# Decays from GpSimd differences and ScalarE exponentials in place of VectorE scans, and split-precision input projections, in a four-batch attention and state-space kernel

## The chip, the core and the metric

The kernel runs on one core of a Trainium2 chip. The metric is the device time of one execution in microseconds (us), as the median of three runs. In the profile PE is TensorE's matmuls, PEld its weight loads, DVE is VectorE, ACT is ScalarE, POOL is GpSimd and SP is SyncE, which here only issues DMAs.

## The reference, cut to what matters

Everything is float32. The input is four batches of 128 channels by 32x32 pixels, so 1024 tokens a batch. Two blocks follow each other:

```python
# block 1: attention over the 1024 tokens of a batch
h = group_norm(x, gn_w, gn_b)                       # 8 groups
q, k, v = split(einsum('bnc,oc->bno', tokens(h), qkv_w) + qkv_b)
attn = softmax(einsum('bnc,bmc->bnm', q, k) / sqrt(128))
x = image(einsum('bnm,bmc->bnc', attn, v) @ proj_w.T + proj_b) + x

# block 2: a state-space layer with 4 heads of 32 and a state of 64
u = layernorm(tokens(x))
zxbcdt = einsum('bld,ed->ble', u, in_w)             # z 128, xBC 256, dt 4
dt = softplus(zxbcdt[..., -4:] + dt_bias)
xBC = silu(causal_conv4(xBC) + conv_b); xs, Bm, Cm = split(xBC)
A = -exp(A_log)
def step(state, inp):                               # 1024 steps
    dA = exp(dt_t * A)
    state = state * dA + (dt_t * x_t) * B_t
    y_t = einsum('bhpn,bn->bhp', state, C_t)
y = (ys + Dp * xs) * silu(z)
y = y * rsqrt(mean(y * y) + EPS) * rms_w
out = y @ out_w.T
x = x + image(out) * sigmoid(se2(relu(se1(mean_pixels(out)))))
```

## The kernel before

The four batches are called a, b, c and d. Attention of one batch and the state-space layer of the batch before it are interleaved in one instruction stream per engine. The order of all steps of all engines is one long list, `ORDER`, written out by hand; each engine walks the list and does the steps that are its own, so each engine's queue is a part of that list, in that order. A step's name is its kind, its number, its batch and, after an @, the PSUM bank that it fills: `InX1c@4` is the second half of the x projection of batch c, in bank 4.

**Attention** of a batch has 8 query tiles of 128 tokens. `S` makes the scores of a query tile against half of the keys, by three products of rounded operands: the float32 operands are split into a part rounded to fp32r and what is left (`h_hi`, `h_lo`, `q_hi`, `q_lo`), and high by high, high by low and low by high are added in PSUM. `max` (VectorE), `exp` (ScalarE), `T` (four transposes on TensorE), `pT` (ScalarE copies them out) and `PV` (TensorE, float32) follow, then `inv`, `res` and `stats` on VectorE.

**The state-space layer** works on halves of 512 tokens (n is 0 or 1) and on chunks of 128 tokens, four to a half. `u_tok` (ScalarE) normalizes, `UT` transposes, and `u` (ScalarE) copies the bank to SBUF. `InX`, `InBC` and `InZ` are one float32 product each of the weights `winC` and a half of `u`, 512 columns wide. `Dt` makes dt for four chunks by four float32 products with `u` as the weights and 128 columns of `winC` moving, of which the last four count. `dt_x` adds the bias (VectorE), `sp_exp` and the nine `sp` steps are the softplus and the log decay `la` of each token and head. `conv_x` is a convolution on VectorE, `conv_bc` one on GpSimd with terms from ScalarE.

**The decays.** Within a chunk the scan is turned into a product with a matrix L of 128 by 128 decays for each head, L[s, i] being the decay from token s to token i, and 0 where i is before s. `Cum` sums `la` up to each token on TensorE. For batches a, b and c (`by_dma(b)`): `dA` holds the decay of each token (with the first one forced to 0 by the bias `first`), and `dec` the exponential of the sums; `DAT` transposes both, `rows` copies them to SBUF, `wr` writes them to DRAM, and eight `bc` DMAs a batch read each chunk's rows back, spread over all 128 partitions, into L. There `l` turns a chunk into the matrix by one scan on VectorE (multiply by the decay, add the identity). For batch d the same matrix comes from three fp32r products into a bank (`L`: rows, minus columns, and `below`, which holds -32768 where i is before s) and an exponential on ScalarE. `to_end` takes the last column, `xend` (GpSimd) weighs the inputs, `U` and `st` make the states, `m` multiplies L by the bank of `G`, and `Y` applies it. The next batch's L is read in once `Y` of the batch before is done.

The steps that the text speaks of, as they stand in the step functions of each engine:

```python
                elif kind == "l" and by_dma(b):          # VectorE, before
                    chunk = L[:, HEADS * n:HEADS * (n + 1), :].rearrange("p a b -> p (a b)")
                    wait(dve, spread[n], b, 16)
                    V.tensor_tensor_scan(chunk, chunk, ident4[:, :, :].rearrange("p a b -> p (a b)"), 0.0, ALU.mult, ALU.add
                                         ).then_inc(l_ready.sem, 1)
```

Of the kernel before, what the change touches and what calls it, by code (L numbers as in the profile page):

```python
# [5 lines left out]
F32 = mybir.dt.float32  # L6
# [5 lines left out]
P = 128  # L12
# [21 lines left out]
FIRST_BIAS = -1000.0  # L34
# [28 lines left out]
masks0 gn_stats0 warm3 gn_mm10@4 kq_mm@0 gn_dev0 gn_mm20 gn_ve0 kq_ev warm5 gn_pow0 gn_aff0 h_hi0a h0a h1a h_lo0a  # L63
h_hi1a vp_mm@2 Q0a@4 q_hi0a vp_ev V0a@2 xob0a v0a q_lo0a V1a@1 h_lo1a S0a S1a Q1a@2 win_s win_mm@4 xob1a v1a max0a
exp0a gn_bs1 T0a@0 S2a exp1a S3a alog T1a@3 pT0a masks1 max1a PV0a pT1a PV1a exp2a T2a@0 S4a win_ev exp3a inv0a q_hi1a
res0a pT2a S5a stats0a T3a@3 q_lo1a max2a pT3a gn_bs2 PV2a PV3a gn_bs3 exp4a T4a@0 S6a exp5a S7a T5a@1 inv1a pT4a
gn_stats1 res1a pT5a max3a exp6a gn_mm11@3 exp7a PV4a PV5a S8a T6a@0 stats1a pT6a S9a T7a@2 gn_dev1 inv2a pT7a res2a
max4a PV6a PV7a exp8a stats2a inv3a xob0b exp9a T8a@2 S10a T9a@4 res3a pT8a S11a stats3a PV8a pT9a ln_ve0a gn_mm21
PV9a max5a ln_pow0a u_tok0a gn_ve1 exp10a UT0a@2 exp11a u0a S12a S13a gn_pow1 max6a T10a@3 inv4a pT10a Dt0a@1 exp12a
gn_aff1 dt_x0a exp13a T11a@4 InBC0a@0 res4a h0b sp_exp0a h1b sp0a S14a InX0a@3 S15a h_hi0b sp1a h_lo0b pT11a raw_bc0a  # L70
h_hi1b PV10a T12a@2 stats4a conv_bc0a Q0b@4 PV11a V0b@1 max7a h_lo1b inv5a exp14a q_hi0b exp15a q_lo0b sp2a sp3a
T13a@0 sp4a S0b sp5a pT12a res5a raw_x0a pT13a Q1b@4 S1b max0b q_hi1b PV12a term0a conv_x0a T14a@3 exp0b exp1b sp6a
pT14a T15a@0 PV13a q_lo1b S2b sp7a pT15a conv_x1a S3b T0b@4 inv6a stats5a sp8a T1b@0 res6a term1a max1b exp2b PV14a
PV15a exp3b inv7a pT0b stats6a Cum0a@3 S4b dec0a res7a stats7a ln_ve1a T2b@4 ln_pow1a conv_x2a S5b h0c dA0a pT1b V1b@2
conv_x3a InZ0a@0 v0b pT2b max2b u_tok1a PV0b exp4b conv_bc1a exp5b UT1a@4 S6b S7b v1b PV1b conv_bc2a u1a cd0a term2a
T3b@1 conv_bc3a DAT0a@3 Dt1a@4 max3b exp6b pT3b inv0b zv0a exp7b S8b dt_x1a T4b@2 InBC1a@4 sp_exp1a rows0a zt0a S9b
res0b PV2b max4b sp9a wr0a pT4b T5b@2 wo_s th_bc0a InX1a@3 th_x0a PV3b gate0a exp8b exp9b T6b@1 inv1b xob1b silu0a
S10b raw_bc1a sp10a pT5b stats0b sp11a res1b h1c sp12a pT6b S11b PV4b sp13a T7b@2 raw_x1a conv_bc4a pT7b sp14a T8b@1
max5b exp10b exp11b bc0a pT8b PV5b sp15a l0a T9b@3 sp16a c0a S12b conv_x4a bc1a inv2b term3a res2b S13b xob0c sp17a
# [1357 lines left out]
```

## Time and profile before

| | |
|---|---|
| median of 3 runs | 271.45 us (271.21 to 271.54) |
| the profiled execution's own time | 272.0 us |
| its span, first to last instruction | 269.8 us |
| mean granted TensorE clock | 0.993 of full speed |
| busy: PE, DVE, ACT, POOL | 254.5, 223.4, 208.1, 115.8 us |

The span is what the trace covers; 2.2 us of the execution lie outside it. Busy time is the union of an engine's instructions. Instructions of one engine overlap by some ten nanoseconds each, so the mean of one times their count is more than the busy time of an engine. Matmuls are pipelined and their ends are modelled, so how fast TensorE gets through its work is read from the chain of waits, which goes from end to end.

### The profile page before, as it was taken

The page shows a single profiled execution, that of the slowest core. Times are in us where ns is not written, and L with a number is a line of the kernel's source. Part 1 is how long each engine was busy: PE and PEld are TensorE (multiplying, and loading weights), DVE is VectorE, ACT ScalarE, POOL GpSimd, SP SyncE. Part 2 cuts the span into 40 slices and gives each one's busy share as a digit, 9 for nine tenths or more (in the row PEclk, how much of TensorE's full clock was granted, in tenths as well). Part 3 has the DMA queues.
Part 4 walks back from the last instruction along what each step waited for, and adds up shares of the span by engine and source line. Part 5 has one row for each costly group of instructions (what it writes and reads, how often), then busy time and mean ns, then how long its engine had stood idle before and what let it go on. Part 6 is the DMA issues. An engine that isn't in the chain of part 4 may idle for free. (4 is left out here: it accounts for less than half of the span.)

```text
span 269.8 us, 6198 instructions
## 1 busy us (share of the span) xinstructions
PE 254.5 (94%) x1992; PEld 224.3 (83%) x1992; DVE 223.4 (83%) x516; ACT 208.1 (77%) x414; POOL 115.8 (43%) x114
## 2 busy tenths in 40 slices
PE   2999999999999999999999999999999999989791
PEld 2989997998899889988899789888988798777680
DVE  4689746565598498999999999999989999799933
ACT  2347577989999875898887799767988889998361
POOL 8010021206402730235289742572286269758440
PEclk9999999999999999999999999999999999999997
DMA  6930000000040340000133300051005100101103
GB/s 177 395 145 4 0 0 4 2 0 0 11 149 5 108 129 2 0 2 0 38 125 112 126 2 0 6 173 64 0 2 193 45 4 2 39 0 42 39 4 117
DMA packets 10987, 15.29 MB, mean 57 GB/s; under 512 B 1515, under 2 KB 5708, under 8 KB 10956
## 3 DMA queue, kind: packets, MB, share of 16 engines
q1 hardware_dynamic: 10412, 14.69, 16.2%
q8 instruction: 17, 0.28, 0.4%
q10 hardware_dynamic: 544, 0.21, 0.3%
q14 instruction: 14, 0.11, 0.1%
HBM read 12.70 MB, written 2.20 MB: 55 GB/s over the span
## 5 line engine op out<-in xcount | busy, mean ns | idle before, releaser
L1169 PE MATMUL attn_out<-values,pT 128*128 128x129 f32 x512 | 65.6, 275 | 0.1
L1169 PEld LDWEIGHTS attn_out<-values,pT 128*128 128x128 f32 x512 | 62.6, 191 | 3.6 <-issue 1.7
L986 DVE TENSOR_REDUCE neg_max<-scores 128x1 f32<-128x1024 f32 x32 | 39.0, 1219 | 16.1 <-PE scores L1169 16.0
L655 ACT ACTIVATE probs<-scores,neg_max 128x512 f32<-128x512 f32 x64 | 42.4, 684 | 9.1 <-DVE neg_max L986 9.0
L661 ACT ACTIVATE pT<-bank 128x512 f32<-128x512 f32 x64 | 37.6, 594 | 14.0 <-PE bank L1247 13.9
L1247 PE MATMUL bank<-ident,probs 128*128 128x128 f32 x256 | 37.7, 273 | 0.0
L1247 PEld LDWEIGHTS bank<-ident,probs 128*128 128x128 f32 x256 | 30.3, 141 | 4.5 <-issue 1.4
L1169 PE MATMUL scores<-h_hi,q_hi 128*128 128x512 f32 x64 | 31.7, 496 | 0.0
L567 POOL TENSOR_TENSOR ln_rstd<-ln_var,neg_half 128x4 f32<-128x4 f32 x8 | 11.3, 1412 | 45.5 <-DVE ln_var L1008 45.5
L1079 DVE TENSOR_TENSOR_SCAN L<-L,ident 128x512 f32<-128x512 f32 x24 | 30.4, 1274 | 0.0
L581 POOL TENSOR_TENSOR pre<-pre,th 128x512 f32<-128x512 f32 x16 | 22.6, 1410 | 15.1 <-ACT pre L687 8.2
L1169 PE MATMUL scores<-h_hi,q_lo 128*128 128x512 f32 x64 | 25.2, 394 | 0.0
L1169 PE MATMUL scores<-h_lo,q_hi 128*128 128x512 f32 x64 | 25.1, 393 | 0.0
L1169 PE MATMUL bank<-u,winC 128*128 128x512 f32 x48 | 24.0, 596 | 0.0
L1093 DVE TENSOR_TENSOR L<-L,bank 128x512 f32<-128x512 f32 x32 | 20.8, 677 | 0.4 <-PE bank L1169 0.3
L1025 DVE SCALAR_TENSOR_TENSOR pre<-raw,vec,pre 128x512 f32<-128x512 f32 x21 | 18.6, 884 | 0.0
L588 POOL TENSOR_TENSOR xend<-xdt,to_end 128x512 f32<-128x512 f32 x8 | 8.9, 1108 | 20.9 <-DVE xdt L1072 12.7
L561 POOL TENSOR_TENSOR h_lo<-h,h_hi 128x512 fp32r<-128x512 f32 x6 | 8.5, 1420 | 21.7 <-ACT h_hi L638 21.7
L594 POOL TENSOR_TENSOR xs<-y,gate 128x512 f32<-128x512 f32 x7 | 9.8, 1406 | 14.2 <-DVE y L1134 14.2
L1169 PEld LDWEIGHTS scores<-h_hi,q_hi 128*128 128x128 f32 x64 | 12.2, 190 | 3.4 <-issue 1.8
L599 POOL TENSOR_TENSOR y_rstd<-ms,neg_half 128x4 f32<-128x4 f32 x8 | 10.4, 1306 | 10.1 <-DVE ms L1137 10.1
L1169 PEld LDWEIGHTS scores<-h_lo,q_hi 128*128 128x128 f32 x64 | 12.2, 190 | 2.6 <-issue 1.9
(219 smaller groups left out, 597.2 us busy)
## 6 DMA issues: line engine op xcount, KB each, us to landing
L<-decay_rows_d SPq DMA_DIRECT2D x24, 256.0 KB, 3.8
res<-in_x_tok SPq DMA_DIRECT2D x4, 512.0 KB, 7.9
out<-res SPq DMA_DIRECT2D x8, 256.0 KB, 2.0
x_all<-in_x SPq DMA_DIRECT2D x3, 512.0 KB, 8.6
decay_in<-decay_rows_d SPq DMA_DIRECT2D x24, 64.0 KB, 3.4
x_all<-in_x SPq DMA_DIRECT2D x2, 256.0 KB, 3.2
winT<-in_in_wT SPq DMA_DIRECT2D x1, 194.0 KB, 7.1
wqkv<-in_qkv_w ACTq DMA_DIRECT2D x1, 192.0 KB, 4.0
```

The source lines that it names most:

```text
L567: pool.tensor_tensor(ln_rstd[:, four], ln_var[:, four], neg_half[:, four], ALU.pow).then_inc(ln_rstd_ready.sem, 1)
L581: pool.tensor_tensor(pre[:, 1, half_of(n)], pre[:, 1, half_of(n)], term(b, n, j), ALU.add).then_inc(tap["bc"].sem, 1)
L594: pool.tensor_tensor(y2[:, half], y[:, half], gate[:, half], ALU.mult).then_inc(y2_ready.sem, 1)
L599: pool.tensor_tensor(y_rstd[:, four], ms[:, four], neg_half[:, four], ALU.pow).then_inc(y_rstd_ready.sem, 1)
L655: act.activation(probs[:, i % 2, half_of(h)], scores[:, half_of(h)], ACT.Exp, bias=neg_max[:, i:i + 1]).then_inc(exp_done.sem, 1)
L661: act.activation(pT[:, i % 2, QUAD * h:QUAD * (h + 1), :], bank[:, :].rearrange("p (a b) -> p a b", a=QUAD), ACT.Copy).then_inc(pT_ready.s ...
L986: V.tensor_reduce(neg_max[:, n:n + 1], scores[:, :], AX.X, ALU.max, negate=True).then_inc(max_ready.sem, 1)
L1025: V.scalar_tensor_tensor(pre[:, 0, half_of(n)], raw[:, 0, n * HALF + j:(n + 1) * HALF + j], vec[:, CONV_X + j:CONV_X + j + 1], pre[:, 0, h ...
L1079: V.tensor_tensor_scan(chunk, chunk, ident4[:, :, :].rearrange("p a b -> p (a b)"), 0.0, ALU.mult, ALU.add).then_inc(l_ready.sem, 1)
L1093: V.tensor_tensor(M[:, HEADS * n:HEADS * (n + 1), :], L[:, HEADS * n:HEADS * (n + 1), :], bank[:, tile(c)].unsqueeze(1).broadcast_to([P, H ...
L1169: return T.matmul(o, w, v, start=start, stop=stop)
L1247: last = T.transpose(bank[:, tile(c)], probs[:, i % 2, tile(QUAD * h + c)], ident[:, :])
```

## The change

For batches a, b and c the VectorE scan `l` is replaced. The rows spread into L are now the running sums and not the decays: `dA` copies them out of the `Cum` bank, as it did for batch d. A new step `ld` on GpSimd does two passes over a chunk: it subtracts the sum at s and adds `below`. `l` is then an exponential on ScalarE. The projections use rounded parts: `u_hi` (the old `u`, written as fp32r), `u_lo` (a new VectorE step, the bank minus `u_hi`, held for one half only), `win_hi` and `win_lo`. Each of `InX`, `InBC`, `InZ` is three fp32r products of 512 columns instead of one float32 product. `Dt` is eight fp32r products with the tokens as weights and 8 or 4 columns moving instead of four float32 products of 128 columns, and `dt_x` has a second addition. The transposed bank is now released by `u_lo`. `wqkv` shares SBUF with `zv`. `ORDER` is new as a whole (left out here; it has the same steps and the 32 new ones); no DMA is added or removed.

```diff
@@ VectorE @@
-                    for h in range(HEADS):
-                        V.tensor_copy(ident4[:, h, :], ident[:, :])
...
-                    V.tensor_scalar(first[:, :], ident[:, 0:1], FIRST_BIAS, None, ALU.mult)
...
-                    V.tensor_copy(winC[:, :], bank[:, 0:INPROJ])
+                    step_done(V.tensor_copy(win_hi[:, :], bank[:, 0:INPROJ]))
+                    step_done(V.tensor_tensor(win_lo[:, :], bank[:, 0:INPROJ], win_hi[:, :].bitcast(F32), ALU.subtract))
+                    V.tensor_copy(win_dt[:, 0:HEADS], win_hi[:, 3 * P:INPROJ].bitcast(F32))
+                    V.tensor_copy(win_dt[:, HEADS:2 * HEADS], win_lo[:, 3 * P:INPROJ].bitcast(F32))
...
+                elif kind == "u_lo":
+                    wait(dve, u_hi_ready, b, n + 1)
+                    for use in ("InX", "InBC", "InZ", "Dt"):
+                        wait(dve, filled[use], b - 1, n + 2)
+                    bank = take(dve, b, "UT", n)
+                    V.tensor_tensor(u_lo[:, :], bank[:, :], u_hi[:, half].bitcast(F32), ALU.subtract).then_inc(u_lo_ready.sem, 1)
                 elif kind == "dt_x":
...
+                    V.tensor_tensor(by_head, parts[:, :, HEADS:2 * HEADS], by_head, ALU.add).then_inc(dtx_ready.sem, 1)
...
-                elif kind == "l" and by_dma(b):
-
-                    chunk = L[:, HEADS * n:HEADS * (n + 1), :].rearrange("p a b -> p (a b)")
-                    wait(dve, spread[n], b, 16)
-                    V.tensor_tensor_scan(chunk, chunk, ident4[:, :, :].rearrange("p a b -> p (a b)"), 0.0, ALU.mult, ALU.add
-                                         ).then_inc(l_ready.sem, 1)
@@ GpSimd @@
+                elif kind == "ld":
+                    wait(pool, spread[n], b, 16)
+                    wait(pool, dA_ready, b, n // QUAD + 1)
+                    pool.wait_ge(below_ready.sem, 1)
+                    chunk = L[:, HEADS * n:HEADS * (n + 1), :]
+                    c = n % QUAD
+                    pool.tensor_tensor(chunk, chunk, dA[:, n // QUAD, HEADS * c:HEADS * (c + 1)].unsqueeze(2)
+                                       .broadcast_to([P, HEADS, P]), ALU.subtract).then_inc(ld_step.sem, 1)
+                    wait(pool, ld_step, b, n + 1)
+                    pool.tensor_tensor(chunk, chunk, below[:, :].bitcast(F32).unsqueeze(1).broadcast_to([P, HEADS, P]), ALU.add
+                                       ).then_inc(ld_ready.sem, 1)
@@ ScalarE @@
-                    act.activation(u[:, half], bank[:, :], ACT.Copy).then_inc(u_ready.sem, 1)
+                    act.activation(u_hi[:, half], bank[:, :], ACT.Copy).then_inc(u_hi_ready.sem, 1)
...
-                    if by_dma(b):
-                        act.activation(dA[:, n, 0:R], la[:, n, :], ACT.Exp, bias=first[:, :], scale=1.0 / A_SCALE
-                                       ).then_inc(dA_ready.sem, 1)
-                    else:
-
-                        bank = take(act, b, "Cum", n)
-                        act.activation(dA[:, n, 0:R], bank[:, 0:R], ACT.Copy, scale=1.0 / A_SCALE).then_inc(dA_ready.sem, 1)
+                    wait(act, ld_ready, b - 1, QUAD * (n + 1))
+                    bank = take(act, b, "Cum", n)
+                    act.activation(dA[:, n, 0:R], bank[:, 0:R], ACT.Copy, scale=1.0 / A_SCALE).then_inc(dA_ready.sem, 1)
...
-                elif kind == "l" and not by_dma(b):
+                elif kind == "l" and by_dma(b):
+                    wait(act, ld_ready, b, n + 1)
+                    chunk = L[:, HEADS * n:HEADS * (n + 1), :]
+                    act.activation(chunk, chunk, ACT.Exp).then_inc(l_ready.sem, 1)
+                elif kind == "l":
@@ TensorE @@
-                    mm(bank[:, :], winC[:, tile(k)], u[:, half]).then_inc(done, 1)
+                    mm(bank[:, :], win_hi[:, tile(k)], u_hi[:, half], True, False)
+                    mm(bank[:, :], win_lo[:, tile(k)], u_hi[:, half], False, False)
+                    wait(pe, u_lo_ready, b, n + 1)
+                    mm(bank[:, :], win_hi[:, tile(k)], u_lo[:, :], False, True).then_inc(done, 1)
...
                     for c in range(QUAD):
-                        last = mm(bank[:, tile(c)], u[:, tile(QUAD * n + c)], winC[:, INPROJ - P:INPROJ])
+                        at = c * P
+                        mm(bank[:, at:at + 2 * HEADS], u_hi[:, tile(QUAD * n + c)], win_dt[:, :], True, False)
+                        last = mm(bank[:, at:at + HEADS], u_lo[:, tile(c)], win_dt[:, 0:HEADS], False, True)
```

## Rows read from the trace of the kernel before

**Rows 1.** The page's first part: busy us, share of the span, instructions.
```profile
PE 254.5 (94%) x1992; PEld 224.3 (83%) x1992; DVE 223.4 (83%) x516; ACT 208.1 (77%) x414; POOL 115.8 (43%) x114
```

**Rows 2.** Busy time by stretch: us, PE, PEld, DVE, ACT, POOL, clock, DMA share, GB/s.
```profile
76.00:214.00 138.00, 137.56 (x1103) 121.40 (x1102) 129.40 (x274) 115.78 (x234) 63.14 (x47) 1.00 0.19 60
...
255.00:270.00 15.00, 7.66 (x87) 6.89 (x86) 6.49 (x14) 5.42 (x14) 4.54 (x4) 0.87 0.14 54
```

**Rows 3.** The chain of waits from 154 to 206 us: start, us, what.
```profile
156.33 0.68 PE scores L1169 x3
157.01 0.86 PE bank L1169 x2
...
160.53 0.89 PE bank L1169 x8
...
183.47 1.01 PE bank L1169 x32
...
205.26 0.39 PE bank L1169 x4
```

**Rows 4.** TensorE in order of time at the same places.
```profile
156.85 1.02 PE L1169 MATMUL bank<-u,winC 128*128 128x512 f32 x2
...
205.10 0.55 PE L1169 MATMUL bank<-ones,o_sum 128*128 128x1 f32 x4
```

**Rows 5.** VectorE's groups from 76 to 214 us: busy us, mean ns, idle before.
```profile
L1079 DVE TENSOR_TENSOR_SCAN L<-L,ident 128x512 f32<-128x512 f32 x24 | 30.4, 1274 | 0.0
...
L1025 DVE SCALAR_TENSOR_TENSOR pre<-raw,vec,pre 128x512 f32<-128x512 f32 x15 | 14.1, 938 | 0.0
...
L847 DVE TENSOR_TENSOR sp_s<-sp_s,dte 128x16 f32<-128x16 f32 x4 | 0.7, 165 | 0.0
```

**Rows 6.** VectorE in order of time, 145 to 149 us.
```profile
145.32 2.22 DVE L1079 TENSOR_TENSOR_SCAN L<-L,ident 128x512 f32<-128x512 f32 x1
147.46 1.70 DVE L1025 SCALAR_TENSOR_TENSOR pre<-raw,vec,pre 128x512 f32<-128x512 f32 x1
```

**Rows 7.** GpSimd in order of time, 127 to 150 us, idle and its releaser in brackets.
```profile
133.55 1.28 POOL L594 TENSOR_TENSOR xs<-y,gate 128x512 f32<-128x512 f32 x1 [5.17 <-DVE y L1134]
...
138.60 1.92 POOL L567 TENSOR_TENSOR ln_rstd<-ln_var,neg_half 128x4 f32<-128x4 f32 x1 [1.12 <-DVE ln_var L1008]
140.50 2.05 POOL L581 TENSOR_TENSOR pre<-pre,th 128x512 f32<-128x512 f32 x1
142.52 1.27 POOL L555 TENSOR_TENSOR res<-res,ob_row 128x512 f32<-128x512 f32 x1
...
145.19 1.26 POOL L561 TENSOR_TENSOR h_lo<-h,h_hi 128x512 fp32r<-128x512 f32 x1
146.41 2.19 POOL L594 TENSOR_TENSOR xs<-y,gate 128x512 f32<-128x512 f32 x1
```

**Rows 8.** Groups of the whole span that the new instructions are costed by.
```profile
L709 ACT ACTIVATE th<-pre 128x512 f32<-128x512 f32 x8 | 5.0, 629 | 0.6 <-DVE pre L1025 0.6
...
L982 DVE SCALAR_TENSOR_TENSOR q_lo<-bank,col,q_hi 128x512 fp32r<-128x512 f32 x8 | 5.9, 742 | 2.3 <-ACT q_hi L644 2.3
...
L1012 DVE TENSOR_TENSOR dtx<-bank,dtb 128x16 f32<-128x16 f32 x8 | 1.3, 166 | 2.0 <-PE bank L1169 2.0
...
L588 POOL TENSOR_TENSOR xend<-xdt,to_end 128x512 f32<-128x512 f32 x8 | 8.9, 1108 | 20.9 <-DVE xdt L1072 12.7 <-DVE to_end L1088 7.0 <-issue 1.0
```

**Rows 9.** Who waited for whom, whole span: us in total, times, longest.
```profile
ACT pT L661 <- PE bank L1247: 13.9, 19, 2.6
...
ACT probs L655 <- DVE neg_max L986: 9.0, 13, 2.0
```

**Rows 10.** The chain of waits from 228 to 246 us.
```profile
232.43 0.19 DVE dtx L1012
...
239.13 0.18 ACT dA L747
...
240.32 3.65 PE bank L1169 x26
```

More of the change, by code:

```diff
@@ L62 @@
 ORDER = """
[L63 to L67, printed above, removed]
@@ L128 @@
[L128 to L132 removed]
+masks0 warm3 gn_stats0 gn_mm10@0 kq_mm@1 gn_dev0 gn_mm20 gn_ve0 kq_ev gn_pow0 warm5 gn_aff0 vp_mm@0 h0a h_hi0a win_s
@@ new lines @@
+h_lo0a h_hi1a alog Q0a@1 q_hi0a h1a vp_ev h_lo1a q_lo0a V0a@4 S0a S1a win_mm@0 v0a masks1 max0a gn_bs1 V1a@3 exp0a
+xob0a exp1a v1a xob0b S2a S3a T0a@3 T1a@4 pT0a max1a exp2a Q1a@2 PV0a pT1a win_ev S4a PV1a inv0a res0a T2a@4 exp3a S5a
+T3a@3 pT2a q_hi1a max2a PV2a xob1b pT3a exp4a gn_bs2 PV3a inv1a T4a@4 gn_bs3 res1a S6a exp5a S7a gn_stats1 max3a pT4a
+T5a@0 PV4a pT5a exp6a q_lo1a gn_mm11@3 PV5a T6a@0 exp7a pT6a stats0a S8a S9a gn_dev1 inv2a T7a@4 res2a max4a pT7a
+stats1a exp8a PV6a PV7a exp9a stats2a T8a@2 pT8a S10a T9a@0 inv3a pT9a S11a xob0c res3a gn_mm21 stats3a PV8a ln_ve0a
@@ new lines @@
+yo_dx1c zt0d c0d Y1c@4 conv_x3d UT1d@2 bt0d dA_rows0d DAT0d@1 Out0c@3 u1d y1c th_x0d dA_T0d L0d@4 Dec0d@1 u_lo1d
+Dt1d@0 o0c decay0d InX1d@3 xs0d g1c fin0b sq1c dt_x1d l0d sp_exp1d L1d@0 os0c Ss1c@1 raw_x1d sp9d InBC1d@4 sp10d l1d
+sp11d XsT0d@0 conv_x4d L2d@3 gate0d sp12d ms1c raw_bc1d term3d conv_bc4d sp13d conv_x5d sp14d L3d@1 l2d sp15d G0d@4
+sp16d conv_x6d l3d y_pow1c sp17d Cum1d@2 dec1d InZ1d@3 xdt0d dA1d to_end0d dA_rows1d conv_bc5d term4d cd1d zt1d m0d
+xend0d DAT1d@0 store0b dA_T1d m1d zv1d Out1c@2 term5d U0d@1 conv_x7d st0d o1c conv_bc6d L4d@3 L5d@0 L6d@2 conv_bc7d
@@ L210, in build @@
         winTg = sb("winTg", [P, INPROJ])
-        winC = sb("winC", [P, INPROJ])
+        win_hi, win_lo = sb("win_hi", [P, INPROJ], F32R), sb("win_lo", [P, INPROJ], F32R)
+        win_dt = sb("win_dt", [P, 2 * HEADS], F32R)
         dtb = sb("dtb", [P, HEADS])
@@ L241, in build @@
         u_tok = sb("u_tok", [P, TILES, P])
-        u = sb("u", [P, TOKENS])
+        u_hi, u_lo = sb("u_hi", [P, TOKENS], F32R), sb("u_lo", [P, HALF], F32R)
         raw = sb("raw", [P, 2, PAD + TOKENS])
@@ L267, in build @@
         dA = sb("dA", [P, 2, P])
-        first = sb("first", [P, 1])
         decay_rows = sb("decay_rows", [2 * R, 2, P])
@@ L372, in released @@
         def released(kind, n, b):
-            one = {"V": v_ready, "T": pT_ready, "UT": u_ready, "InX": raw_ready["x"], "InBC": raw_ready["bc"], "Dt": dtx_step,
+            one = {"V": v_ready, "T": pT_ready, "UT": u_lo_ready, "InX": raw_ready["x"], "InBC": raw_ready["bc"], "Dt": dtx_ready,
                    "XsT": xdt_ready, "BT": BT_ready, "U": st_ready, "Yo": yo_ready, "Y": y_ready, "Ss": ms_ready,
```

151 lines of the change are left out of this document (74 added, 77 removed).

## The prediction

> **What bounds the kernel now.** I read the page's first part, then busy time by stretch, then the chain of waits, then the groups. TensorE is busy 254.5 of 269.8 us [rows 1]. From 76 to 214 us, the stretch that holds all 24 scans of `l`, it is busy 137.6 of 138, VectorE 129.4, ScalarE 115.8 and GpSimd 63.1 [rows 2]. Matmuls overlap, so a busy TensorE could still be waiting; the chain of waits decides. From 154 to 206 us it is nearly all TensorE, at the same pace for the same work each time [rows 3]: the kernel's middle is bound by TensorE's work. At about 136 to 149 us it is not: GpSimd works there instruction behind instruction, and the gated product `xs<-y,gate` that `Ss` needs comes last in its queue [rows 7]. From 232 to 240 us one half of batch d is a dependent chain, from `dt_x` through the softplus to `dA` [rows 10], and after 255 us TensorE is busy only half of the time [rows 2].
>
> **In projections.** One float32 product of 512 columns is two instructions and 0.86 us on the chain; the three fp32r products of a score tile are 0.68 [rows 3, 4]. The new projection is three such products. I take 0.70, as a score tile that follows a float32 group may cost: 24 x (0.86 - 0.70) = **-3.8 us**. Bounds: -4.3 at 0.68, and -2.9 (0.74) if now and then the third product waits for `u_lo`.
>
> **Dt.** Eight instructions of 128 columns take 0.89 us now [rows 3]. Eight with 8 or 4 columns are new, each with 128 columns of weights to load. The nearest row is the four of one column, `o_sum`: 0.39 [rows 3, 4], so 0.78 for eight: 8 x (0.78 - 0.89) = **-0.9 us**. Bounds: 0 (the weight load sets the pace whatever moves) and -5.1 (the pace of 32 products with 32 columns of weights, 1.01 us [rows 3], 0.25 for eight). I take the row with full weights.
>
> The Trainium skill, "TensorE: Matmul & The Clock Gate", section LDWEIGHTS, gives a load P/1.2 ns, 107 ns for 128 columns, whatever the type; by it eight take 0.86 us, the term is -0.2 instead of -0.9, and the sum below would be 0.7 us higher. Rows show 98 ns for one-column instructions.
>
> **VectorE.** It loses 24 scans, 30.4 us [rows 5], and four copies of `ident4` in the first microseconds, before its data have landed (0). It gains eight `u_lo`, a subtraction from a bank like `q_lo`, at 742 ns: 5.9 us, and eight additions like `dtx` at 166 ns: 1.3 us [rows 8]. In the stretch 129.4 becomes some 103. It was not what TensorE waited for on the chain, so I take 0 for the relief as such.
>
> **ScalarE.** 24 exponentials from SBUF to SBUF, at 629 ns like the tanh (5.0 us busy for 8, so 0.62 each [rows 8]): 15.0 us, less 0.7 for six `dA`, which become copies. In the stretch 115.8 + 14.3 = 130.1 of some 134 us. Hidden behind TensorE: **0**, but the cover is 4 us thin (rival A). Bounds 0 and the whole 14.3.
>
> **GpSimd.** 24 x 2 passes. The second is like a full addition, 1.27 us; the first has a broadcast operand like `xend`, 1.11 [rows 7, 8]: 24 x 2.38 = 57 us. The stretch goes from 63 to 120 of 134. Behind each `ld` in the same queue stand `conv_bc`, `ln_pow`, `g` (which `Ss` and `Out` need), `xend` and `y_pow`. Each chunk of L also comes later: 2.4 + 0.6 us instead of 1.27, and a half of four chunks takes GpSimd 9.5 us. A batch has some 55 us of TensorE time, mostly attention of the next batch, that covers this. **0**, bounds -3 and +9 (rivals C and B).
>
> **The two engines' common path.** At 145.32 a scan takes 2.22 us, not 1.2: GpSimd's `h_lo` began at 145.19 and ends at 146.45. GpSimd's `xs` then starts at 146.41 and takes 2.19 instead of 1.28, to just after the scan's end, and the next convolution tap on VectorE takes 1.70 [rows 6, 7]. Instructions of both engines with two operands in SBUF go in turns, and with some 0.15 us of overlap at each handover. The scan was one of these; both passes of `ld` are too, and `u_lo` is not (one operand is a bank). In the stretch 15 VectorE groups of this kind, the first with 30.4 us, the last with 0.7 [rows 5], sum to 70 us, and GpSimd has 63: 133 of 138. The change takes 30 away and adds 57.
>
> The Trainium skill, "SBUF — State Buffer", section Who interferes with whom, has this as a rule: a VectorE instruction with two SBUF inputs and a GpSimd one that reads SBUF exclude each other, and the second "fully blocks" until the first ends. The trace agrees (2.22 instead of 1.2 us), except for the 0.15 us at a handover. By the rule without that overlap the stretch needs 160 us of a path that offers 134; rival B is what it would do.
>
> **The end.** Batch d keeps its decays. But `u_lo1d` comes between `u_hi` and `Dt1d`, and the second addition before the softplus, on the chain of [rows 10]: 0.74 + 0.17 = **+0.9 us**. Bounds 0 (if the new order starts it earlier) and +1.5 with waits.
>
> **Start.** `win_lo` and `win_dt` are four small VectorE instructions beside the first scores: 0. `win_s` now stands before `h_lo0a`, and could hold it for its DMA: 0 to +0.8; I take 0, since two V products no longer come before the first scores.
>
> **Sum.** 269.8 - 3.8 - 0.9 + 0.9 = 266.0 us of span. 2.2 us lie outside it: 268.2. The profiled execution is at 272.0, 0.55 above the median, so I forecast 267.6 for the median; a measurement tells 0.2%, 0.5 us, from no change.
>
> **Rivals.**
> A. *ScalarE becomes the bound.* It makes exponentials and copies that TensorE waits for next, and it waits itself: 13.9 us for transposes and 9.0 for maxima over the span [rows 9]. In the stretch it was idle 22.2 us. If more than 4 us of that stays, ScalarE decides. If half stays (11.1), the stretch is 130.1 + 11.1 = 141.2, 3.2 longer than before. Outside of it 1.5 of the projections' gain and +0.9 remain: 271.45 + 3.2 - 1.5 + 0.9 = **274.0**. For it: 97% load. Against: VectorE carried 94% here without stalling TensorE.
> B. *GpSimd's queue and the common path.* Without waits counted twice (24 scans at 1.2, 15 taps at 0.74 and GpSimd's at 1.27 take some 16 us off the 133), the path needs 117 - 29 + 57 = 145 us where 138 were. +7, and outside -0.6: **278**. Decisive once GpSimd's queue in the stretch passes 134. Against: the power steps are long but read four elements, and handovers overlap; `ld` can also spread beyond the stretch.
> C. *More gain.* On the chain at 138 to 148.6 us GpSimd's own waits for VectorE are 0.9 (`ln_pow`), 0.8, 0.9 and, for a power step between, 0.4 over what such instructions take alone [rows 7]. Without scans 3 us of this go, and a lighter VectorE delivers `y` and `ln_var` sooner: **264.6**, down to 262.
> D. *Nothing is seen.* The order changes, stalls of 4 us come with the thin ScalarE cover and use up the projections' gain: **271.4**.
>
> **How the numbers follow.** Forecast 0.45 (its own range 265.5 to 269.5), C 0.20, D 0.08, A 0.16, B 0.11. Faster by over 0.2% are the forecast, C and a little of D and A: 0.68; within 0.2%: 0.08; slower 0.24. The range holds 8 in 10 if it runs from 262.5 to 274.5: C almost whole, A whole, and B left out.
>
> **What would show it.** Three fp32r products with `u_hi` and `u_lo`, 0.70 us a group on the chain; `Dt` 0.78 for eight; 24 exponentials at 0.6 us; 48 passes at 1.1 and 1.3 us or, where turns are taken, up to 2.2; convolution taps on VectorE above 0.94; TensorE's busy time in 76 to 214 still near 100%. Wrong if ScalarE's busy time is above 96% over a long stretch while TensorE idles (A), if GpSimd's is (B), or if TensorE's chain in the middle is the same length although each projection is shorter (D).

## The result, and the profile after

The kernel after takes **274.12 us** (median of 4 runs, 273.77 to 274.48); the kernel before, on the same chip, 271.5. The ratio is 1.0082, 95% interval 1.0046 to 1.0119: slower by 2.6 us where 3.9 us faster was forecast. Ratios here are over undisturbed runs only, so they can differ a little from a ratio of the medians. The spans of the profiled executions are 272.0 and 269.8 us; 1.8 and 2.2 us of the executions lie outside them.

The page's first part of the kernel after, beside [rows 1]:

```profile
PE 253.1 (93%) x2016; PEld 228.3 (84%) x2016; DVE 226.0 (83%) x506; ACT 218.6 (80%) x438; POOL 167.9 (62%) x162
```

30.4 us of scans are gone from VectorE and 7 us of `u_lo` and additions have come; of the 223.4 us before, 200 should be left. It is busy 226.0, more than before. That is the first thing to explain. Busy time by stretch, beside [rows 2] (us, PE, PEld, DVE, ACT, POOL, clock, DMA share, GB/s):

```profile
76.00:214.00 138.00, 134.62 (x1111) 123.02 (x1109) 123.24 (x260) 124.79 (x254) 112.29 (x91) 1.00 0.20 62
```

VectorE 123.2 instead of the 103 of the forecast; TensorE no longer 100% (134.6 of 138). VectorE's groups over the whole span (busy us, mean ns of one, idle before):

```profile
L862 DVE TENSOR_TENSOR sp_s<-sp_s 128x112 f32<-128x112 f32 x8 | 6.1, 757 | 0.1
L864 DVE TENSOR_TENSOR_SCAN sp_sum<-sp_s,sp_coef 128x128 f32<-128x128 f32 x8 | 6.0, 748 | 0.1
L1027 DVE TENSOR_TENSOR u_lo<-bank,u_hi 128x512 fp32r<-128x512 f32 x8 | 5.5, 690 | 2.5 <-ACT u_hi L687 2.4
...
L859 DVE TENSOR_TENSOR sp_s<-sp_s,dte 128x16 f32<-128x16 f32 x8 | 4.8, 594 | 0.2
L855 DVE TENSOR_SCALAR sp_den<-dte 128x16 f32<-128x16 f32 x8 | 4.0, 497 | 1.6 <-ACT dte L744 1.6
L875 DVE TENSOR_SCALAR la<-la_raw 128x16 f32<-128x16 f32 x8 | 3.7, 463 | 0.1
...
L1035 DVE TENSOR_TENSOR dtx<-bank,dtx 128x16 f32<-128x16 f32 x8 | 1.4, 175 | 0.3
L1032 DVE TENSOR_TENSOR dtx<-bank,dtb 128x16 f32<-128x16 f32 x8 | 1.3, 167 | 0.8 <-PE bank L1183 0.7
```

`sp_s<-sp_s,dte` has 16 columns and took 165 ns [rows 5]; it now takes 594. Nine of the ten groups of the softplus, which touch SBUF alone, take 1.3 to 3.6 times what they took; the tenth, the reciprocal, takes the same (242 and 246 ns). Together they are busy 39 us where they were busy 20. `dtx`, of the same size but with a bank as an operand, is where it was (166 and 167 ns; its new second addition takes 175), and `u_lo`, also from a bank, takes 690, less than the 742 that it was costed at. VectorE and then GpSimd in order of time show what holds the small ones up:

```profile
152.04 0.24 DVE L857 RECIPROCAL sp_s<-sp_den 128x16 f32<-128x16 f32 x1
152.31 1.30 DVE L859 TENSOR_TENSOR sp_s<-sp_s,dte 128x16 f32<-128x16 f32 x1
153.65 1.07 DVE L862 TENSOR_TENSOR sp_s<-sp_s 128x112 f32<-128x112 f32 x1
154.64 1.21 DVE L998 TENSOR_REDUCE neg_max<-scores 128x1 f32<-128x1024 f32 x1
```

```profile
150.82 1.40 POOL L591 TENSOR_TENSOR L<-L,dA 128x512 f32<-128x512 f32 x1
152.30 1.27 POOL L594 TENSOR_TENSOR L<-L,below 128x512 f32<-128x512 f32 x1
153.53 1.05 POOL L601 TENSOR_TENSOR xend<-xdt,to_end 128x512 f32<-128x512 f32 x1
```

The product of 16 columns starts at 152.31, the mask's pass at 152.30: it ends at 153.61, just behind the pass (153.57), after 1.30 us instead of 0.17. The next small one, at 153.65, does the same with `xend`. Behind them waits the maximum of a score tile, which the exponentials, the transposes and TensorE wait for in turn. I add up, for all of VectorE's instructions that read and write SBUF alone, with one input or with two, the time beyond the shortest fifth of their form: 12.2 us before, **32.4 us** after. This sum is called VectorE's waits from here on; how the forms are grouped moves it by about 1 us, alike in all versions. Nearly all of the rise is in the softplus.

TensorE's own work went as forecast for the projections, though not for `Dt`. In order of time:

```profile
140.75 0.63 PE L1261 MATMUL bank<-ident,probs 128*128 128x128 f32 x4
141.13 0.48 PE L1183 MATMUL bank<-u_hi,win_hi 128*128 128x512 f32 x1
141.45 0.40 PE L1183 MATMUL bank<-u_hi,win_lo 128*128 128x512 f32 x1
141.68 0.40 PE L1183 MATMUL bank<-u_lo,win_hi 128*128 128x512 f32 x1
...
145.33 0.25 PE L1183 MATMUL bank<-win_dt,u_hi 128*128 128x8 f32 x1
...
146.12 0.25 PE L1183 MATMUL bank<-win_dt,u_lo 128*128 128x4 f32 x1
```

A projection runs from the end of the transposes (141.38) to 142.08, 0.70 us. The eight small products of `Dt` start 0.79/7 = 0.113 us apart, so eight take 0.90. Taking TensorE's work as the sum of the usual distances between the ends of its products, it went from 237.1 to 233.5 us (-3.6), and what its ends lag behind that went from 22 to 28. Both figures rest on modelled ends and on how the products are grouped, so they are good to 1 or 2 us. By the rows above and [rows 3], the projections alone save 24 x (0.86 - 0.70) = 3.8 us. So the saving came, and more stalls than it. GpSimd's and ScalarE's new groups:

```profile
L594 POOL TENSOR_TENSOR L<-L,below 128x512 f32<-128x512 f32 x24 | 33.6, 1401 | 1.9
L591 POOL TENSOR_TENSOR L<-L,dA 128x512 f32<-128x512 f32 x24 | 26.6, 1109 | 10.3 <-DMA L<-decay_rows_d 10.3
```

```profile
L768 ACT ACTIVATE L<-L 128x512 f32<-128x512 f32 x24 | 15.1, 638 | 0.3 <-POOL L L594 0.3
```

### The profile page after: what moved, and what is told of

Read it like the earlier page. It is cut to its first block and busy times, and to the rows that moved or that the text cites. A ratio compares the mean times of both kernels' runs of the same rounds, so it can differ in the third digit from the quotient of the medians.

```text
span 272.0 us, 6372 instructions
## 1 busy us (share of the span) xinstructions
PE 253.1 (93%) x2016; PEld 228.3 (84%) x2016; DVE 226.0 (83%) x506; ACT 218.6 (80%) x438; POOL 167.9 (62%) x162
## 5 line engine op out<-in xcount | busy, mean ns | idle before, releaser
L594 POOL TENSOR_TENSOR L<-L,below 128x512 f32<-128x512 f32 x24 | 33.6, 1401 | 1.9
L591 POOL TENSOR_TENSOR L<-L,dA 128x512 f32<-128x512 f32 x24 | 26.6, 1109 | 10.3 <-DMA L<-decay_rows_d 10.3
L569 POOL TENSOR_TENSOR ln_rstd<-ln_var,neg_half 128x4 f32<-128x4 f32 x8 | 9.4, 1178 | 35.2 <-DVE ln_var L1020 35.2
L1183 PE MATMUL scores<-h_hi,q_hi 128*128 128x512 f32 x64 | 28.5, 445 | 0.2 <-ACT probs L668 0.2
L583 POOL TENSOR_TENSOR pre<-pre,th 128x512 f32<-128x512 f32 x16 | 21.2, 1325 | 8.2 <-ACT pre L700 4.6
L1183 PE MATMUL scores<-h_hi,q_lo 128*128 128x512 f32 x64 | 25.4, 397 | 0.1
L1183 PE MATMUL scores<-h_lo,q_hi 128*128 128x512 f32 x64 | 25.2, 393 | 0.0
L1045 DVE SCALAR_TENSOR_TENSOR pre<-raw,vec,pre 128x512 f32<-128x512 f32 x21 | 17.7, 843 | 0.1
L601 POOL TENSOR_TENSOR xend<-xdt,to_end 128x512 f32<-128x512 f32 x8 | 10.2, 1274 | 10.3 <-DVE to_end L1102 3.9
L768 ACT ACTIVATE L<-L 128x512 f32<-128x512 f32 x24 | 15.1, 638 | 0.3 <-POOL L L594 0.3
L1183 PEld LDWEIGHTS scores<-h_hi,q_lo 128*128 128x128 f32 x64 | 12.0, 188 | 3.2 <-DVE q_lo L994 0.5
L700 ACT ACTIVATE pre<-raw,vec 128x512 f32<-128x512 f32 x16 | 13.2, 825 | 0.0
```

The lines of the kernel that those rows point to most:

```text
L583: pool.tensor_tensor(pre[:, 1, half_of(n)], pre[:, 1, half_of(n)], term(b, n, j), ALU.add).then_inc(tap["bc"].sem, 1)
L591: pool.tensor_tensor(chunk, chunk, dA[:, n // QUAD, HEADS * c:HEADS * (c + 1)].unsqueeze(2) .broadcast_to([P, HEADS, P]), ALU.subtract).th ...
L594: pool.tensor_tensor(chunk, chunk, below[:, :].bitcast(F32).unsqueeze(1).broadcast_to([P, HEADS, P]), ALU.add).then_inc(ld_ready.sem, 1)
L700: act.activation(pre[:, k, half], raw[:, k, half], ACT.Identity, scale=vec[:, at:at + 1], bias=vec[:, at + TAPS:at + TAPS + 1]).then_inc(t ...
L768: act.activation(chunk, chunk, ACT.Exp).then_inc(l_ready.sem, 1)
L1045: V.scalar_tensor_tensor(pre[:, 0, half_of(n)], raw[:, 0, n * HALF + j:(n + 1) * HALF + j], vec[:, CONV_X + j:CONV_X + j + 1], pre[:, 0, h ...
```

## Experiments on GpSimd's passes

The diffs from here on are shortened: semaphores and declarations are left out.

**Passes that read nothing.** In the kernel after both passes of `ld` become five memory sets of nearly the same total length (2.30 us a chunk instead of 2.51), so the decays are left out:

```diff
-pool.tensor_tensor(chunk, chunk, dA..., ALU.subtract)
-pool.tensor_tensor(chunk, chunk, below..., ALU.add)
+for k in range(4):
+    pool.memset(chunk, 0.0)              # each waits for the one before
+pool.memset(chunk[:, 0, :], 0.0)
```

> The changed kernel with the two GpSimd passes of each ld replaced by five memsets of the same chunk, which take about the same GpSimd time (2.2 to 2.4 us a chunk) and read no SBUF; L then holds zeros, so the decays are left out. Path theory: VectorE no longer waits for them; its small softplus instructions fall back to their lengths alone, its busy time from 226 to 205-210 us, and the time to 268 to 271. ScalarE theory and order theory: VectorE's waits were hidden, 273.5 to 274.5 as it is. GpSimd's queue as the bound: also unchanged, as its load is.

268.28 us (268.24 to 268.76), ratio 0.9868 (0.9834 to 0.9902). GpSimd is busy 163.1 us, 4.8 less than in the kernel after; VectorE's waits fall from 32.4 to 17.3 us. The page's first part, then VectorE's group of the example above:

```profile
PE 250.7 (94%) x2016; PEld 227.9 (85%) x2016; DVE 212.3 (80%) x506; ACT 217.9 (82%) x438; POOL 163.1 (61%) x234
```

```profile
L857 DVE TENSOR_TENSOR sp_s<-sp_s,dte 128x16 f32<-128x16 f32 x8 | 1.4, 172 | 0.2
```

The same order, the same ScalarE and TensorE work, nearly the same queue, and 5.8 us less. Some 0.5 us of it may be the shorter queue: that is my estimate, from the version with four subtractions below, where 33 us more of GpSimd's passes go with 3.2 us. The rest is the price of the reads. What is left is 3.2 us faster than before, near the forecast (267.6): the kernel after loses its gain, and more, to GpSimd's reads.

The memory sets are not free for VectorE either. In order of time, VectorE and then GpSimd:

```profile
157.76 0.16 DVE L871 TENSOR_TENSOR la_raw<-dt,a_neg 128x16 f32<-128x16 f32 x1
157.96 0.36 DVE L873 TENSOR_SCALAR la<-la_raw 128x16 f32<-128x16 f32 x1
```

```profile
157.18 1.11 POOL L591 MEMSET L<- 128x512 f32 x2
```

A product with two inputs runs beside the memory set at its own length. The one-input instruction behind it, 0.17 us when alone, ends at 158.32, just behind the memory set (158.29). `sp_den` does the same in this run (354 ns), `la` and the copy `to_end` in the run with memory sets in the old order (501 and 431 ns). So VectorE's two-input instructions wait for GpSimd's reads, and its one-input `TENSOR_SCALAR` and `COPY` also for its writes; the reciprocal waits for neither (at most 0.25 us in the kernel after, with up to 1.3 us of an addition left). By kind, VectorE's waits for one-input instructions are some 5 us with either form of `ld`; the fall is in the others.

**The same in the kernel before.** There, 24 further GpSimd passes, one behind each decay step of the first three batches, once as sums of two views of the identity, once as three memory sets of together 1.36 us; nobody reads the result. Scans, projections and the rest stay (the set-up weights share space with `gate` to make room).

```diff
+elif kind == "gx":
+    pool.tensor_tensor(idle[:, :, :], view, view, ALU.add)     # view: ident, broadcast to 512 columns
```
```diff
+elif kind == "gx":
+    for width in (2, HEADS, HEADS):
+        pool.memset(idle[:, 0:width, :], 0.0)
```

> The kernel before with 24 more GpSimd passes of 512 columns (the sum of two views of the identity, written to a place that nobody reads), one behind each decay step of the first three batches, and the set-up weights in shared space. It is the price of GpSimd's work in the old order, with VectorE's scans kept. Waits over SBUF as the cause: VectorE's waits rise by 24 x 0.4 to 0.8 = 10 to 19 us less what GpSimd waits instead, and the time by 2 to 6, to 273.5 to 277.5. If GpSimd's passes are free as long as the queue has room (43% busy): 271.5 to 272.

> The same as the run before with each added pass as three memory sets of together 1.3 us: the same time on GpSimd's queue at the same places, nothing read from SBUF. If the cost is the waits over SBUF, 271.3 to 272.3; if it is GpSimd's queue that makes its later work late, the same as the run before.

Reads: 287.24 us (ratio 1.0565, 1.0538 to 1.0592). Memory sets: 277.95 (1.0238, 1.0222 to 1.0255). First the page's line of the reads, then that of the memory sets:

```profile
PE 259.9 (91%) x1992; PEld 227.1 (80%) x1992; DVE 237.3 (83%) x516; ACT 208.9 (73%) x414; POOL 143.7 (50%) x138
```

```profile
PE 256.7 (93%) x1992; PEld 225.8 (82%) x1992; DVE 224.5 (81%) x516; ACT 208.5 (75%) x414; POOL 143.6 (52%) x186
```

GpSimd is busy 143.6 to 143.7 us in both; the reads alone cost 9.3 us, and VectorE's waits are 25.4 against 14.9. Both expectations were too low, and the second shows what I had not expected: 6.4 to 6.6 us for 33 us of work in a queue that is 43% busy before [rows 1]. Work in the queue has a price even where nothing is read. Part of it is that what stands behind it comes later, as this row of the waits with memory sets shows, which the kernel before does not have:

```profile
PE bank L1200 <- POOL h_lo L586: 2.2, 1, 2.2
```

How much of it is that, and how much the one-input instructions that wait for the memory sets, was not taken apart.

**One input instead of two.** The mask is put on with an affine select, the result is the same:

```diff
-pool.tensor_tensor(chunk, chunk, below..., ALU.add)
+pool.affine_select(out=chunk, in_=chunk, compare_op=ALU.is_ge, fill=-BELOW, base=0,
+                   pattern=[[0, HEADS], [1, P]], channel_multiplier=-1)
```

> The kernel after with GpSimd's second pass (the addition of the mask, two inputs) written as an affine select, one input, that puts the same -32768 in the same places: the result is the same. In the set-up such a select took 0.29 to 0.38 us for 128 columns, so 0.9 to 1.4 us for 512, about as long as the pass it replaces. That VectorE's waits come from GpSimd passes with two inputs from SBUF: VectorE's waits fall from 32 us by a third to a half and a third to a half of the 5.8 us come back, 271 to 272.5. If any read of SBUF by GpSimd holds VectorE up: no change, 274, less only by what the select is shorter.

271.51 us median (269.39 to 274.25 over 11 runs), ratio 0.9978 (0.9952 to 1.0005): about 1% or 2.8 us faster than the kernel after, and not to be told from the kernel before. GpSimd's two groups:

```profile
L591 POOL TENSOR_TENSOR L<-L,dA 128x512 f32<-128x512 f32 x24 | 26.6, 1109 | 9.2 <-DMA L<-decay_rows_d 9.2
...
L594 POOL TENSOR_SCALAR_AFFINE_SELECT L<-L 128x512 f32<-128x512 f32 x24 | 17.9, 744 | 3.6
```

The select takes 744 ns where the addition took 1401, which I had not foreseen (0.9 to 1.4), and VectorE's waits are 24.7 (the profile is of the longest of the 11 runs, 274.25 us). Both the length and the inputs changed, so the times do not say whether one input holds VectorE up less than two. The trace does, VectorE and then GpSimd:

```profile
161.07 0.40 DVE L871 SCALAR_TENSOR_TENSOR dt<-dtx,sp_log 128x16 f32<-128x16 f32 x1
```

```profile
160.81 0.63 POOL L594 TENSOR_SCALAR_AFFINE_SELECT L<-L 128x512 f32<-128x512 f32 x1
```

`dt` takes 0.15 to 0.18 us alone and here ends at 161.47, just behind the select (161.44). In this run and the next, six two-input instructions of VectorE start well inside a select, and all six end 23 to 27 ns behind it. So the select holds VectorE up as an addition does; what helps is that it is half as long. The next version has the subtraction as four instructions of one input and a number per partition:

```diff
+for h in range(HEADS):
+    pool.tensor_scalar(chunk[:, h, :], chunk[:, h, :], dA[:, n // QUAD, at:at + 1], None, ALU.subtract)
```

> As the one before, and the first pass as well: four GpSimd subtractions of one number per partition from 128 columns in place of one subtraction with two inputs of 512 columns, same result. Passes with two inputs as the cause: near the run with memory sets, 268.5 to 270.5, if the four take about as long as the one (1.11 us). If they are much longer (over 1.6 us), GpSimd's queue becomes late and it gives part back, 270 to 274. Any read as the cause: 274 or more.

274.73 us, ratio 1.0139 (1.0095 to 1.0183). The row:

```profile
L593 POOL TENSOR_SCALAR L<-L,dA 128x128 f32<-128x128 f32 x96 | 61.7, 660 | 8.1 <-DMA L<-decay_rows_d 8.1
```

Four take 2.6 us instead of 1.1. VectorE's waits are 21.6 although the passes are on for 33 us longer than in the version with the select alone. In the trace, two-input instructions of VectorE that start inside such a subtraction, with 0.35 to 0.56 us of it left, take 0.16 to 0.29 us: it holds them up a little or not at all. But GpSimd is busy 186 us, and the longer queue costs more than that gives.

**The select first**, so that `dA` is needed only by the second pass:

> The kernel after with the select as GpSimd's first pass, on the landed rows, and the subtraction of the row decays as its second: the same result and the same work as the select version (269.4 to 272.2), but one fewer wait ahead of the first pass. If that wait matters: 269 to 270; if not, as the select version, 270 to 271.5.

271.77 us, ratio 1.0029 (0.9992 to 1.0066): no better than the select behind the subtraction. Waiting for `dA` ahead of the first pass costs nothing that can be measured.

**One pass, and the column's decay as the bias of the exponential** (the mask is still put on by GpSimd):

```diff
-pool.tensor_tensor(chunk, chunk, dA..., ALU.subtract)
+for h in range(HEADS):
+    act.activation(chunk[:, h, :], chunk[:, h, :], ACT.Exp, bias=dA[:, n // QUAD, at:at + 1], scale=-1.0)
```

> The kernel after with one GpSimd pass over each chunk of decays instead of two: the decay of the row is stored negated, GpSimd only puts the mask on, and the exponential takes the column's decay as its bias, four exponentials of 128 columns instead of one of 512. GpSimd has 24 x 1.1 = 27 us less, all of it reading SBUF; ScalarE has 24 x (4 x 0.28 - 0.63) = about 12 us more. That GpSimd's passes over SBUF make VectorE wait: about half of the 5.8 us that all passes cost comes back, so 269 to 271.5. ScalarE as a bound would take it back: 275 to 280.

280.71 us, ratio 1.0317 (1.0252 to 1.0382): where 269 to 271.5 was expected if the reads alone decide, and 275 to 280 if ScalarE does. VectorE's waits fall to 25.2 us, but the exponentials are twice what they were:

```profile
L767 ACT ACTIVATE L<-L,dA 128x128 f32<-128x128 f32 x96 | 30.7, 409 | 0.1
```

ScalarE is busy 232.4 instead of 218.6. Its spare time is as thin as rival A said: 14 us more of it, with 27 us of GpSimd's passes gone, make the kernel 6.6 us slower than the kernel after.

**Less of ScalarE.** Was it the bound already in the kernel after? Exponentials of 4 of the 512 columns:

```diff
-act.activation(chunk, chunk, ACT.Exp)
+act.activation(chunk[:, :, P - 1:P], chunk[:, :, P - 1:P], ACT.Exp)
```

> The changed kernel with the 24 exponentials over L taken of 4 columns of 512 (the last of each head), the rest of L left as logarithms, so the decays are wrong there. ScalarE loses some 10 us of its 218.6. ScalarE theory (rival A): 270 to 271.5. Path theory: ScalarE was covered, 273 to 274.3.

276.18 us median (273.53 to 278.29), ratio 1.0121 (1.0066 to 1.0176); ScalarE is busy 209.7 (in the profiled run, the longest, 278.29 us). 9 us less of it bring no gain. The run with memory sets says the same from the other side: ScalarE is busy 129.2 of 138 us there in the stretch, and TensorE 137.7.

## Experiments on the projections and on VectorE's length

**Parts in the old order.** The kernel before with the new projections, `Dt` included, `u_lo` at its full size, a step of its own behind `u`; scans and order stay.

```diff
-mm(bank[:, :], winC[:, tile(k)], u[:, half])
+mm(bank[:, :], win_hi[:, tile(k)], u_hi[:, half], True, False)
+mm(bank[:, :], win_lo[:, tile(k)], u_hi[:, half], False, False)
+mm(bank[:, :], win_hi[:, tile(k)], u_lo[:, half], False, True)
```

> The kernel before, in its old order and with its VectorE scans, and only the projections by rounded parts (u_lo inserted behind u, held for both halves, weights of the set-up sharing space). TensorE does 3.6 us less work, VectorE gets 5.5 us of u_lo. If the loss of the whole change is the decays' doing (path theory: GpSimd's passes over L make VectorE's instructions with two SBUF operands wait), this gains: 268.5, between 267 and 270. If u_lo and the second addition at the end and the waits for u_lo eat what the products save, it is 271 to 273.

277.31 us, ratio 1.0218 (1.0172 to 1.0264), where 267 to 270 was expected: with TensorE's work down as in the kernel after, 5.7 us slower than before. The waits have a row for it, of TensorE for `u_lo` (us, times, longest):

```profile
PE bank L1204 <- DVE u_lo L1042: 3.3, 3, 1.3
```

Two more versions take `u_lo` apart: 16 of its 512 columns, and no `u_lo` at all (the third product reads `u_hi`, so the low part of `u` is left out; no wait, no step).

```diff
-V.tensor_tensor(u_lo[:, half], bank[:, :], u_hi..., ALU.subtract)
+V.tensor_tensor(u_lo[:, n * HALF:n * HALF + R], bank[:, 0:R], u_hi..., ALU.subtract)
```
```diff
-wait(pe, u_lo_ready, b, n + 1)
-mm(bank[:, :], win_hi[:, tile(k)], u_lo[:, half], False, True)
+mm(bank[:, :], win_hi[:, tile(k)], u_hi[:, half], False, True)
```

> The kernel before with the projections by parts in its own order, as in the first experiment, but the subtraction that forms u_lo runs over 16 of 512 columns (the other columns of u_lo are zeros written in the set-up, so the low part of u is left out of most of the product). TensorE does the same work; VectorE has 8 x (0.69 - 0.1) = 4.7 us less. That VectorE bounds beside TensorE: the 4.7 us come back nearly whole, 277.3 - 4 to 277.3 - 6, so 271 to 273; if TensorE's 3.6 us then count as well, down to 268. The rival, that the projections' third product waiting for one more step costs the time whatever its length: 276 to 277.5.

> The kernel before with the projections by parts, but no u_lo at all: the third product reads u_hi again (so the low part of u is left out of the result), TensorE does the same work as with parts, and nobody waits for u_lo or holds the bank for it. If the forecast's term of -3.8 us is on the path: 268 to 269 (3.6 less than before, about 0.5 of the second addition back). If TensorE's saving is not on the path: 271 to 272.

273.95 us (1.0087, 1.0048 to 1.0126) and 273.25 us (1.0045, 1.0018 to 1.0073). `u_lo`'s length costs some 3.4 of the 5.7 us. But even with no `u_lo`, TensorE's saving does not arrive: its work is 4.1 us less than before (233.0), its lag 27.3 instead of 22. Neither expectation held.

**No `u_lo` in the kernel after**, the same edit:

> The same on the kernel after: no u_lo, the third product reads u_hi. It prices u_lo in the new order: VectorE has 5.5 us less. VectorE with its waits as a bound there: 268.5 to 271.5. Nothing on the path: 273.5 to 274.5.

273.18 us (1.0103, 1.0046 to 1.0159): 0.9 us below the kernel after by the medians, not below it by the ratios. In the new order no price of `u_lo` can be told from the noise.

**Scans back.** The kernel after, its order and its projections, with the scans of before:

> The changed kernel in its new order, with the VectorE scans and the exponential of dA back and no ld; the projections stay by parts. GpSimd's busy time falls from 168 to some 105 us, ScalarE's by 15, VectorE's waits from 32 to some 12 us, but the scans add 29. Path theory: VectorE's sum is the same either way (226 + 29 - 20 = 235 busy), so 271 to 275 in an order not made for scans. Order theory (the new order itself is what loses): 274 or more. If neither, as in the old order with parts: 268 to 270.

284.04 us, ratio 1.0438 (1.0396 to 1.0481). That is 9.9 us slower than the kernel after. The new order was laid out for a light VectorE; with the scans back ScalarE waits for maxima 21.8 us (9.0 before [rows 9]):

```profile
ACT probs L659 <- DVE neg_max L993: 21.8, 21, 3.0
```

**Less of VectorE in the kernel before.** Scans over 256 of their 512 columns, and over 16:

```diff
-V.tensor_tensor_scan(chunk, chunk, ident4..., 0.0, ALU.mult, ALU.add)
+V.tensor_tensor_scan(chunk[:, 0:256], chunk[:, 0:256], ident4[:, 0:2, :]..., 0.0, ALU.mult, ALU.add)
```

> The kernel before with the 24 decay scans over 256 of their 512 columns (half of the decays are left as the exponentials of the first column alone), so VectorE has 24 x 0.55 to 0.6 = 13 to 14 us less and nothing else changes. My forecast took VectorE's relief as 0: then 270.5 to 271.5. If VectorE was a bound beside TensorE in the kernel before, a third to two thirds of it comes back: 262 to 267.

> The kernel before with the 24 decay scans over 16 of their 512 columns (so the decays are left out nearly whole): VectorE has 24 x 1.1 = 26 us less and nothing else changes. If VectorE's length is off the path, as the half scans say (-0.4 for 11 us less): 270 to 271.5. If the second half of it counts: 266 to 269.

271.09 us (0.9964, 0.9932 to 0.9996) and 271.16 us (0.9991, 0.9970 to 1.0012). In the second VectorE is busy 21.6 us less:

```profile
PE 254.2 (94%) x1992; PEld 224.7 (83%) x1992; DVE 201.8 (75%) x516; ACT 208.1 (77%) x414; POOL 107.6 (40%) x114
```

and nothing comes of it; VectorE only waits longer for scores (24.0 us by the waits, 16.0 before). The half scans gave 0.4%, at the edge of their interval. By itself VectorE's length was hardly on the path. **Both savings at once:**

> The same with the projections by parts without u_lo (TensorE 3.6 us less; the low part of u left out as well). TensorE and VectorE pacing each other by turns: the two together give what neither gives alone, 265 to 268. A third thing that sets the pace: no less than the better of the two alone, 270 to 273.

269.66 us, ratio 0.9931 (0.9915 to 0.9948), between what I expected of TensorE and VectorE pacing each other (265 to 268) and of a third thing (270 to 273). The parts without `u_lo` are worth +0.45% with the full scans and -0.6% with the short ones: 1.6 of TensorE's 4 us arrive once VectorE is light, none of them while it is not. Through which wait is not shown: ScalarE waits 9.3 us for maxima in both versions.

**Float32 projections in the kernel after**, and in the version with the select:

```diff
-mm(bank[:, :], win_hi[:, tile(k)], u_hi[:, half], True, False)      # and the two behind it
+mm(bank[:, :], winC[:, tile(k)], u[:, half])
```

> The kernel after with the float32 projections of before in place of the parts: no u_lo and no second addition, so VectorE has about 7 us less and TensorE 3.6 us more; decays by GpSimd and ScalarE and the order stay. VectorE with its waits as the bound: faster than after, 268 to 272. TensorE as the bound: 277 to 278.

> The kernel after with the select and the float32 projections of before: VectorE has 7 us less than in the select version, TensorE 3.6 us more. VectorE as the main bound of what is left: 268 to 270. Projections neutral, as they were without the select (275.2 against 274.1): 270.5 to 272.5.

275.18 us (1.0127, 1.0056 to 1.0198) and 274.34 us (1.0105, 1.0072 to 1.0138). With both passes as they are, the parts are worth 0.4% and the intervals overlap; with the select they are worth 1.3%, 3.4 us, TensorE's whole saving; I had expected the float32 version at 268 to 272.5. So the worth of TensorE's saving depends on what the other engines do beside it. What decides it stays open: it is not VectorE's waits alone, which are short in the old order (12.2 us before), where nothing of the saving arrives.

## Why the prediction was wrong

**The step that failed** is the one on the two engines' common path together with the 0 for GpSimd. The prediction saw that passes with both operands in SBUF take turns, counted the path at 117 - 29 + 57 = 145 us where 138 were, and then gave it nothing in the sum; it kept the +7 for rival B, at 0.11. Measured, the version without the reads is 5.8 us faster; the common path cost that much where the sum had 0. It also looked for the cost at the wrong instructions. It named scans and convolution taps, long ones that lose little. The taps did not grow at all (842 ns in the stretch after, 938 before [rows 5]). The cost is in the softplus, ten dependent instructions of 16 to 128 columns per half. Nine of them can meet a pass of 1.1 to 1.4 us and then wait for nearly all of it, so 0.17 us become 0.6 for one of them, and 0.25 become 0.49 on average of the ten. A sum of busy times on the path, 133 of 138 before, cannot show this: what counts is how many VectorE instructions arrive while a pass is on. Not all of VectorE's waits come from the reads: with memory sets 17.3 us are left where the kernel before has 12.2, so some 5 of the 20 us more come with the new order and the memory sets. That the waits reach TensorE through the maxima behind the softplus is what the example shows once; the whole of 5.8 us was not followed there.

**Luck.** The measured 274.12 lies inside the stated range, 262.5 to 274.5, and beside rival A's 274.0. Neither speaks for the prediction: the kernel moved the other way, and A's cause, ScalarE as the bound, is not what the runs show.

The rule of the Trainium skill that stood in the prediction, "SBUF — State Buffer", section Who interferes with whom, is that a VectorE instruction with two SBUF inputs contends with a GpSimd one that reads SBUF, over a shared port pair that it calls "an exclusive lock"; its words "fully blocks" stand there beside VectorE's two-port modes. The example at 152.31 us agrees: 1.30 us for an instruction that takes 0.17 alone.

**VectorE's relief taken as 0** was right in the old order: 21.6 us less of it move the kernel before by 0.1%. It was right only for the relief by itself. Together with TensorE's saving it has a value (1.6 us). So the two terms of the sum were not independent: the 3.8 us of the projections depended on the relief that was entered as 0, and a version that brings only the projections is 0.45% to 2.2% slower.

**In projections**, -3.8 us: a group takes 0.70 as forecast. The term is right as TensorE's work (-3.6 with `Dt`), and arrives whole only in the version with the select.

**Dt**, -0.9 us: measured 0.90 us for eight, the same as before, so 0, the bound that the prediction named. The figure of the Trainium skill, "TensorE: Matmul & The Clock Gate", section LDWEIGHTS, 107 ns for 128 columns of weights, was the better guide; the rows show 113. Its formula names no type, and here eight float32 instructions before and eight fp32r ones after take the same (0.89 and 0.90 us). The one-column row that I chose was too short by 15 ns an instruction.

**ScalarE**, 0: right for the kernel after. 638 ns an exponential (629 forecast), 124.8 us busy in the stretch (130 forecast). Rival A falls: 9 us less of ScalarE give nothing. That its cover is thin is right too: 14 us more make the kernel 6.6 us slower, although GpSimd's passes are halved.

**GpSimd's work**: 2.51 us a chunk where 2.38 was forecast, 60 us in all. In the new order its queue shows no cost of that size: with 55 us of memory sets the kernel is 3.2 us faster than before. In the old order 33 us of memory sets cost 6.6, in spite of 57% of spare time. Whether the order or the missing scans make the difference is not shown: no run puts memory sets into the new order with the scans, or into the old order without them.

**The end**: the time from the last row tile of batch d's attention to the end of the span is 44.0 us before and 46.7 after, +2.7 instead of +0.9. In the kernel before with parts, `u_lo` at full size, it is 44.1: `u_lo1d` and the second addition cost 0.2. It is 46.4 with memory sets, so the rest is neither the path nor `u_lo`; I put it down to the new order, and did not take that apart.

**Rival B** named the right mechanism. Its condition, GpSimd's queue in the stretch above 134 us, did not come true (112.3), and its price was 278: the path decides without the queue being full. Rival C, a gain from a lighter VectorE, did not come: VectorE did not become lighter, and where it did, alone, it gave next to nothing.

**The account**: forecast 267.6; without `Dt`'s gain 268.5; measured without reads 268.3; with the reads' 5.8, 274.1. That the second and third agree is in part luck: the end took 1.8 us more than forecast, so something else, which no run isolates, gave about 2 us.

**What stays open**: through which instruction the last waits reach TensorE in each stretch; what decides whether TensorE's saving arrives; why the parts without `u_lo` make the old order 1.2 us slower rather than leave it as it was; and what of the 6.6 us for memory sets in the old order each instruction behind them takes. No version that computes everything beat both kernels beyond the measurement's doubt. The one with the select is the best of the changed ones: 1% faster than the kernel after, level with the kernel before.

## What to carry to other kernels

Before moving work from VectorE to GpSimd, count the VectorE instructions that work on SBUF alone and will fall beside it, not their busy time: each short one can pay the length of a whole GpSimd pass, and dependent chains of them pay again and again. A saving on one engine of a kernel in which three are busy 75% to 95% is worth what the others let through, so try it alone and with the others' relief before adding terms. Where GpSimd must pass over data, take the form that is shortest (a select for a mask), and price a place in its queue even when the queue is half empty.

## What the hardware showed that I had not expected

- An affine select of 128x512 took 0.74 us on GpSimd, an addition of a broadcast mask to the same tile 1.40, though both write the same tile.
- GpSimd with a number per partition is slow: 0.66 us for 128 columns, against 1.11 for 512 columns with a broadcast operand.
- VectorE's `sp_s<-sp_s,dte` of 16 columns, on average: 172 ns with memory sets, 316 with select and subtraction, 594 with the two passes with two inputs.
- Memory sets of GpSimd hold up VectorE's one-input instructions (`la`, 166 ns alone, 365 beside one; `to_end`, 150 alone, 431), though not its two-input ones.
- Products of 4 or 8 columns by 128 columns of weights start 0.113 us apart, one exponential of 128 columns from SBUF with a bias takes 0.41 us where one of 512 takes 0.64.
